# Scores by 64 keys, split loads of keys, and an earlier state update in a two-layer recurrent kernel

## The reference, cut to what matters

```python
L = jnp.where(tri, jnp.exp(cs[..., :, None] - cs[..., None, :]), 0.0)
scores = jnp.einsum('znid,znjd->znij', Cc, Bc) * L
y_diag = jnp.einsum('znij,znjh->znih', scores, Xc)
states = jnp.einsum('znj,znjd,znjh->zndh', decay_states, Bc, Xc)
...
y_inter = jnp.einsum('znid,zndh,zni->znih', Cc, S_prev, jnp.exp(cs))
```

## Time and profile before

| | before |
|---|---|
| runs shown | 724.49, 726.0, 727.79 us; median 726.0 |
| profiled execution | 725.26 us |
| its span, first to last instruction | 723.5 us |
| PE busy | 710.4 us, 98% of the span, 6956 matmul records |
| PE weight loads busy | 589.6 us, 81% |
| DVE busy | 489.1 us, 68% |
| ACT busy | 343.3 us, 47% |
| POOL busy | 76.2 us, 11% |
| loop round, start to start of its first matmul | 87.1 us |

### The profile page before, as it was taken

One profiled execution on the slowest core, in us unless ns is written; L12 is line 12 of the kernel. 1 busy time (PEld: TensorE's weight loads), 2 busy tenths in 40 slices (PEclk: granted clock), 3 DMA queues, 4 the chain that ended last, 5 costly groups with the idle time before them and its releaser, 6 DMA issues.

```text
span 723.5 us, 17997 instructions
## 1 busy us (share of the span) xinstructions
PE 710.4 (98%) x6956; PEld 589.6 (81%) x6956; DVE 489.1 (68%) x1200; ACT 343.3 (47%) x678; POOL 76.2 (11%) x85
## 2 busy tenths in 40 slices
PE   7999999999999999999999999999999999999998
PEld 5877788877898788886888868888688877888787
DVE  5796779529795388845887558955779538795133
ACT  1423792237911577115862068521693227921690
POOL 6201011100110011100111001110011100111020
PEclk9999999999999999999999999999999999999999
DMA  7910450134401253113611127102360025401370
GB/s 234 408 34 30 121 102 4 16 80 131 84 2 27 77 148 60 14 18 103 141 38 16 41 79 154 25 15 75 103 118 3 15 73 142 80 3 23 114 128 15
DMA packets 122444, 55.93 MB, mean 77 GB/s; under 512 B 104384, under 2 KB 114176, under 8 KB 120832
## 3 DMA queue, kind: packets, MB, share of 16 engines
q1 hardware_dynamic: 122368, 54.76, 31.0%
HBM read 42.35 MB, written 12.40 MB: 76 GB/s over the span
## 4 chain that ended last, share of the span: by engine, by line
PE 81%; DVE 8%; DMA 4%; issue 4%; SPq 1%; POOL 1%; ACT 0%; DVEq 0%; POOLq 0%; ACTq 0%
PE psum L1506 63%; DMA hidB<-b_dram 2%; PE psum L1742 2%; DMA b_dram<-B_turned 1%; PE psum L1615 1%; PE psum L1727 1%; PE psum L1780 1%; PE psum L1585 1%; PE psum L1957 1%; PE psum L1753 1%; PE psum L1648 1%; PE psum L1827 1%; DVE hid L1124 1%; PE psum L1597 1%; SPq L456 1%
## 5 line engine op out<-in xcount | busy, mean ns | idle before, releaser
L608 ACT ACTIVATE BC<-psum 64x256 f32<-64x256 f32 x128 | 81.6, 637 | 1.9 <-PE psum L1506 0.2
L1506 PE MATMUL psum<-xn1T,sb_n_gate 128*128 128x256 f32 x256 | 61.3, 382 | 0.0
L1506 PE MATMUL psum<-xn1T,sb_n_up 128*128 128x256 f32 x256 | 60.5, 379 | 0.0
L1506 PE MATMUL psum<-xnT,sb_f_gate 128*128 128x256 f32 x240 | 58.5, 386 | 0.0
L1506 PE MATMUL psum<-xnT,sb_f_up 128*128 128x256 f32 x240 | 57.6, 382 | 0.7 <-DVE S L1187 0.6
L739 ACT ACTIVATE thFB<-psum 128x512 f32<-128x512 f32 x8 | 4.8, 597 | 103.8 <-PE psum L1506 103.8
L1506 PEld LDWEIGHTS psum<-xn1T,sb_n_gate 128*128 128x128 f32 x256 | 48.0, 190 | 6.8
L1506 PEld LDWEIGHTS psum<-xn1T,sb_n_up 128*128 128x128 f32 x256 | 48.1, 190 | 6.2
L1506 PEld LDWEIGHTS psum<-xnT,sb_f_up 128*128 128x128 f32 x240 | 44.7, 189 | 9.4 <-DVE S L1187 3.0
L1506 PEld LDWEIGHTS psum<-xnT,sb_f_gate 128*128 128x128 f32 x240 | 44.1, 189 | 7.0 <-DVE xnT L1171 0.2
L1506 PE MATMUL psum<-sb_f_down,hid 128*128 128x256 f32 x224 | 49.5, 379 | 0.0
(11 more groups left out here) (261 smaller groups left out, 1458.2 us busy)
## 6 DMA issues: line engine op xcount, KB each, us to landing
cs_row<-cs_dram SPq DMA_DIRECT2D x8, 1024.0 KB, 5.0
x_dram<-gate SPq DMA_DIRECT2D x8, 512.0 KB, 2.8
cs_half<-cs_dram SPq DMA_DIRECT2D x16, 256.0 KB, 5.4
hidB<-x_dram SPq DMA_DIRECT2D x8, 512.0 KB, 5.8
b_dram<-B_turned SPq DMA_DIRECT2D x32, 128.0 KB, 3.2
hidB<-b_dram SPq DMA_DIRECT2D x8, 512.0 KB, 5.3
X<-in_x SPq DMA_DIRECT2D x9, 256.0 KB, 3.4
XT<-in_x_turned SPq DMA_DIRECT2D x8, 256.0 KB, 3.5
```

The lines of the kernel that those rows point to most:

```text
L608: ins = a_.activation(cols[:, par, 2 * pair:2 * pair + 2, :], src[64 * par:64 * par + 64, :, s, :], ACT.Identity)
L1506: ins = t_.matmul(ps(t, name)[first_row:first_row + rows, col:col + n], w, x, start=(k == 0), stop=(k == len(ws) - 1))
```

## The change

- `ssd_scores` computes, for each chunk and s, two products in place of one: the first 64 keys against all 128 queries, and the last 64 keys against the last 64 queries. In even chunks the first 64 keys go to PSUM partitions 0 to 63 and the last to 64 to 127; in odd chunks the two halves are swapped.
- So that the rest agrees, rows of odd chunks are swapped in `cs_pos`, `Xrow` and `Brow` as well: each is loaded by three transfers (even chunks; odd chunks' halves) instead of one. Counts of their semaphores follow.
- POOL's mask becomes three selects: even chunks, odd chunks, and the first 64 partitions of odd chunks; each waits for the one before.
- DVE: `end_args` comes after `level_next(4)` and `level_next(5)` instead of before; a wait for the stored output of the tile before stands ahead of them. `B_decayed` comes after `decayed_scores(0)` and `states_0` instead of before. In the last round the order stays.
- ACT: `gate_tanh` comes before `end_exp` and the first `L_exps`.
- First round, PE: the 30 identity matmuls before the first level product are gone; 28 on four quarters of the array stand after the first half of the first gate projection, before `rank_mix`.

```diff
@@ first lines
+KEY_ROWS = [(slice(0, P), 0, slice(0, P)), (slice(0, 64), 1, slice(64, P)), (slice(64, P), 1, slice(0, 64))]
@@ SP
-                    sp_.dma_start(cs_pos[:, :], cs_dram.rearrange("(c p) -> p c", p=P),
-                                  allow_slow_non_contiguous=True).then_inc(cs_loaded, 16)
+                    pos = cs_dram.rearrange("(c two p) -> p c two", two=2, p=P)
+                    by_two = cs_pos[:, :].rearrange("p (c two) -> p c two", two=2)
+                    for to, r, from_ in KEY_ROWS:
+                        sp_.dma_start(by_two[to, :, r], pos[from_, :, r], allow_slow_non_contiguous=True).then_inc(cs_loaded, 16)
...
-                    sp_.dma_start(Brow.rearrange("p q c d -> p (q c) d"),
-                                  b_dram.rearrange("(c p d) -> p c d", p=P, d=SD)).then_inc(B_rows, 16)
+                    keys = b_dram.rearrange("(c two p d) -> p c two d", two=2, p=P, d=SD)
+                    for to, r, from_ in KEY_ROWS:
+                        sp_.dma_start(Brow.rearrange("p q (c two) d -> p (q c) two d", two=2)[to, :, r, :],
+                                      keys[from_, :, r, :]).then_inc(B_rows, 16)
@@ POOL
-                    g.affine_select(out=cs_row[:, :, :], in_=cs_row[:, :, :], compare_op=ALU.is_ge, fill=NEG, base=0,
-                                    pattern=[[0, NQ * SCH], [1, P]], channel_multiplier=-1).then_inc(cs_masked, 1)
+                    by_two = cs_row[:, :, :].rearrange("p (c two) q -> p c two q", two=2)
+                    for last, r, two, base in ((P, slice(0, P), 0, 0), (P, slice(0, P), 1, 64), (64, slice(0, 64), 1, -64)):
+                        m = by_two[r, :, two, :]
+                        ins = g.affine_select(out=m, in_=m, compare_op=ALU.is_ge, fill=NEG, base=base,
+                                              pattern=[[0, NQ * SCH // 2], [1, P]], channel_multiplier=-1)
+                        if last == P:
+                            did(ins)
+                    ins.then_inc(cs_masked, 1)
@@ ACT
+                    gate_tanh()
                     end_exp()
                     L_exps(0)
-                    gate_tanh()
@@ DVE
-                    end_args()
+                    dve.wait_ge(out_stored, b.count(16, 16))
+                    dve.sem_inc(passed, 1)
                     level_next(a, 4)
                     level_next(a, 5)
+                    end_args()
...
-                    B_decayed()
                     decayed_scores(0)
                     states_0()
+                    B_decayed()
@@ PE, ssd_scores
-                    for s in range(NQ):
-                        r = half_rows(s)
-                        ins[s] = t_.matmul(ps(t, names[s])[:, i * P:(i + 1) * P], Bf[r, c * P:(c + 1) * P],
-                                           Cf[r, c * P:(c + 1) * P], start=True, stop=True)
+                    for first in range(2):
+                        k, at = slice(c * P + 64 * first, c * P + 64 * first + 64), 64 * (first ^ (c % 2))
+                        for s in range(NQ):
+                            r = half_rows(s)
+                            ins[s] = t_.matmul(ps(t, names[s])[at:at + 64, i * P + 64 * first:(i + 1) * P], Bf[r, k],
+                                               Cf[r, c * P + 64 * first:(c + 1) * P], start=True, stop=True)
@@ PE, first round
-                def kept_busy(name, count):
-                    open_bank(a, name)
-                    for _ in range(count):
-                        t_.matmul(ps(a, name)[0:64, 0:32], ident[0:64, 0:64], ident[0:64, 0:32], start=True, stop=True)
+                def kept_busy(names, count):
+                    for name in names:
+                        open_bank(a, name)
+                        pe.sem_inc(passed, 1)
+                    for i in range(count):
+                        e, hf = ((0, 0), (1, 1), (0, 1), (1, 0))[i % 4]
+                        r = slice(64 * e, 64 * e + 64)
+                        t_.matmul(lev_pair[64 * hf:64 * hf + 64, e, 0:32], ident[r, 0:64], ident[r, 0:32], start=True, stop=True)
...
                     half_p(a, 0, "g", 0)
+                    kept_busy(["mix_w", "mix_k"], 28)
                     rank_mix()
...
                     project_p(a, 2, "g")
-                    kept_busy("p2u", 30)
                     level(a, 1)
```

More of the change, by code:

```diff
@@ L430, in one @@
                     sp_.sem_inc(passed, 1)
-                    wait(X_rows, b.count(16, 16))
+                    wait(X_rows, b.count(48, 16))
                     sp_.dma_start(x_dram.rearrange("(q p n) -> p q n", q=NQ, p=P), Xnat).then_inc(X_stored, 16)
@@ L435, in one @@
                     sp_.sem_inc(passed, 1)
-                    wait(cs_loaded, b.count(48, 16))
+                    wait(cs_loaded, b.count(80, 16))
                     wait(cs_rows_loaded, b.count(16, 16))
@@ L447, in one @@
                     wait(X_stored, b.count(16, 32))
-                    sp_.dma_start(Xrow.rearrange("p q c d -> p (q c) d"),
-                                  x_dram.rearrange("(c p d) -> p c d", p=P, d=SD)).then_inc(X_rows, 16)
-                    wait(B_rows, b.count(16, 16))
+                    keys = x_dram.rearrange("(c two p d) -> p c two d", two=2, p=P, d=SD)
+                    for to, r, from_ in KEY_ROWS:
+                        sp_.dma_start(Xrow.rearrange("p q (c two) d -> p (q c) two d", two=2)[to, :, r, :],
+                                      keys[from_, :, r, :]).then_inc(X_rows, 16)
+                    wait(B_rows, b.count(48, 16))
                     wait(B_blocks, b.count(2, 2))
@@ L698, in sums_exp @@
                 def sums_exp():
-                    act.wait_ge(cs_loaded, b.count(48, 64))
+                    act.wait_ge(cs_loaded, b.count(80, 96))
                     steps.did(a_.activation(chunk_dec[:, :], cs_half[:, :].rearrange("p (c w) -> p c w", w=P)[:, :, P - 1],
@@ L1280, in end_args @@
                 def end_args():
-                    dve.wait_ge(cs_loaded, b.count(48, 64))
+                    dve.wait_ge(cs_loaded, b.count(80, 96))
                     did(d.tensor_scalar(cs_col[:, :], cs_pos[:, :], -1.0, None, ALU.mult))
@@ L1295, in B_decayed @@
                     dve.wait_ge(to_end_ready, b.count(1, 1))
-                    dve.wait_ge(B_rows, b.count(16, 32))
+                    dve.wait_ge(B_rows, b.count(48, 64))
                     for s in range(NQ):
@@ L1950, in states @@
                 def states():
-                    pe.wait_ge(X_rows, b.count(16, 32))
+                    pe.wait_ge(X_rows, b.count(48, 64))
                     pe.wait_ge(B_ready, b.count(1, 1))
```

## The result

The change makes the kernel slower: 741.5 us median (736.4 to 743.7, 4 runs) against 725.7 beside it, ratio 1.0205, interval [1.0147, 1.0263]. The forecast was 717.8, in a range of 714.3 to 723.0. The profiled execution took 743.73 us (span 742.0; before 725.26 and 723.5).

What follows compares the result with a forecast made beforehand. PE was taken to bound the loop rounds. Gains of 3.2 (first tile), 7 x 0.49 (scores), 1.5 (stall) and 0.1 (last tile) sum to 8.2 us: profiled 725.26 to 717.1, median 717.8, range 714.3 to 723.0.

Steps and rivals of the forecast that it cites:

- First tile, 3.2 us less: First tile: removing 30 dummy matmuls ends DVE's wait, 3.4 us, less 0.2 for the 28 new ones.
- Scores, 1.99 to 1.50 us: Scores on PE: 64 passes on four quarters replace 32, gaining 0.49 us a round.
- the own-block row: Own-block products, 32 passes on four quarters in 0.75 us: read as 94 ns a pass, waiting passes not holding up others.
- a cut in PE's own work: Loop rounds: PE is busy 87.03 of 87.10 us, so cutting its work was claimed worth its full size.
- the 4% named "issue" on the chain: Share of the span named "issue" on the chain of work that ended last, beside PE 81%, DVE 8%, DMA 4%.
- The stall for states_0, 1.5 us: PE's fourth up projection waits for states_0 to free "kv"; moving B_decayed behind it gains 1.5 us over seven rounds.
- B_decayed to 371.2 (1.16): DVE in the fourth round: B_decayed, moved behind states_0, still takes 1.16 us and ends at 371.2.
- 0.6 us left: Margin by which DVE's results are ready before PE's products within chunks and with the carried state need them.
- Loads, mask, ScalarE's order, the new wait: Three loads for one, POOL's three selects, gate_tanh moved earlier, DVE's wait for the stored output: each claimed to cost nothing.
- Rival 2: Split load of B lands late, so B_decayed on DVE makes PE wait: 733 us, chance 0.06.
- rival 1: Matmuls start strictly in program order, so scores cost 1.0 us more in eight tiles: 729 us, chance 0.07.
- rival 3: First tile keeps its time because the clock falls without the dummies: 721.2 us, chance 0.10.

Runs made afterwards that it cites:

- e15: The kernel before with the first tile's edit and the new VectorE and ScalarE order, but old scores, rows, loads and mask: 720.0 us.
- e7: The kernel before with the first tile's edit alone (28 dummies ahead of the rank products, none before the second up projection): 721.4 us.
- e9: The kernel before with the first tile's edit alone, but 44 dummies instead of 28: 720.6 us.
- e3: The changed kernel with 23 dummy matmuls in the first tile instead of 28: 718.7 us, ratio 0.9906.
- e6: The changed kernel with 96 empty instructions at the head of PE's program: 749.4 us.

## Why the prediction was wrong

- **First tile, 3.2 us less:** right. 3.8 in the changed kernel, 3.6 alone.
- **Scores, 1.99 to 1.50 us:** the size was right to the hundredth, and so was the reading of the own-block row. The failed step is the one before it, that "a cut in PE's own work" is "worth its full size" in the loop rounds. It costed the 64 passes by what the array needs, and the change doubles the instructions of that stretch; the 4% named "issue" on the chain were not followed. With the ends of blocks where 28 dummies put them, 10 to 12 us went into "issue". With 23 the loop rounds keep 2.3 of the 2.9 us (six rounds of 0.49): 519.8 us for all six against 522.1 in e15. A stall of 0.65 in across of the unrolled round takes back most of the rest.
- **The stall for states_0, 1.5 us:** right, 1.4 by e15 against e7, as long as B lands as late as in the kernel before (e9).
- **"B_decayed to 371.2 (1.16)" and "0.6 us left":** the second failed step. I looked at GpSimd's select and not at its product, which in the kernel before starts at 371.36, behind B_decayed (368.75 to 369.91). The new place leaves 0.15 us to it (e3), less than the 0.6 that the sum had towards PE; the stall of 1 us ate that, and the meeting cost 5.6 us in states and some 3 in front of within. Without the stall the step holds (e3: 364.88 to 366.04, no wait behind it).
- **Loads, mask, ScalarE's order, the new wait:** nothing, as forecast. Rival 2 did not come; rival 1 is excluded by 1.50, and rival 3 by e7, where the granted clock reads 1.00 up to the first loop round.
- **Total:** 717.8 is 0.9 from what the same edit gives with 23 dummies, 718.7, and 24 from what it gives with 28. The cause of the loss, ends of instruction blocks in dense runs, was no rival of mine, and the chance of 0.07 for slower was too low.

What stays open: what starts an instruction packet. The packet ahead of the stall in chunk_states starts 0.25 to 0.79 us behind the first score in the six rounds and takes 0.95 to 1.28; PE runs out of instructions 2.07 us behind the first score, so the stall varies with the packet. Between the two stalls of a round lie 250 passes, 500 instructions, and some waits; the trace has two packets there (384.07 and 387.70 in the fourth round).

## What to carry to other kernels

An edit that makes PE's stretch denser, or only shifts the instructions ahead of a loop, can move stalls named "issue" in or out: here five dummy matmuls were worth 23 us, more than the whole change. Before judging such an edit, run it with a few instructions more and less ahead of the loop, and look for "issue" in front of PE lines inside dense runs and for an instruction packet that ends shortly ahead of it. Before moving a VectorE operation whose operands are all in SBUF, find GpSimd's on the same time axis, and count the distance to it as the margin.

## Not expected of the hardware

- Fetching instructions isn't hidden here. The Trainium skill, "Runtime: NRT & Kernel Launch", section "Instruction fetch mechanics", gives blocks of 256 instructions and calls the cost of crossing one mostly hidden; by that the changed kernel would have been near 718. The runs show 0.2 to 1.5 us at a crossing in a dense run of short fp32 matmuls (some 12 ns an instruction), 2.4 at most (e6), and nothing where long passes cover it.
- Empty instructions on PE cost 0.03 us each in the loop (32: 0.9 us) and 0.14 at the head (64: PE's first matmul at 11.89 instead of 2.74). Why they cost more there was not tried.
